# Spline layer of a graph network: features normalised singly, base weights held on chip, second half with banks and Silu buffer of its own, first half of the third norm moved ahead

## The reference

```python
def _layernorm(x, axis=-1, eps=1e-05):
    ...
def _L2_gnn_ref(h, W, a, base_w, spline_w, edge_index):
    ...
    att = ex / den[row]
    agg = jax.ops.segment_sum(att[:, None] * h[col], row, num_segments=N_NODES)
    grid = _grid()
    basis = _b_splines(agg, grid)
    out = jax.nn.silu(agg) @ base_w.T + jnp.einsum('nip,oip->no', basis, spline_w)
    return out
def _L3_gnn_ref(x, w, edge_index):
    ...
    message = jnp.concatenate([x, neighbor_mean], axis=-1)
    weighted = jnp.einsum('of,nf->no', w, message)
    return jax.nn.relu(weighted)
...
x = _layernorm(x + _L1_gnn_ref(...), axis=-1)
x = _layernorm(x + _L2_gnn_ref(x, ...), axis=-1)
x = _layernorm(x + _L3_gnn_ref(x, L3_gnn_w, edge_index), axis=-1)
```

## Time and profile before

| | |
|---|---|
| median of 3 runs | 1746.64 us (1743.93 to 1747.52) |
| the profiled execution | 1744.53 us, its span 1742.6 us |
| PE busy | 1470.6 us, 84% |
| DVE busy | 1321.9 us, 76% |
| ACT busy | 727.0 us, 42% |
| POOL busy | 499.8 us, 29% |
| mean granted clock of TensorE | 0.932 |

### The profile page before, as it was taken

One profiled execution on the slowest core, in us unless ns is written; L12 is line 12 of the kernel. 1 busy time (PEld: TensorE's weight loads), 2 busy tenths in 40 slices (PEclk: granted clock), 3 DMA queues, 4 the chain that ended last, 5 costly groups with the idle time before them and its releaser, 6 DMA issues.

```text
span 1742.6 us, 24098 instructions
## 1 busy us (share of the span) xinstructions
PE 1470.6 (84%) x7759; PEld 794.3 (46%) x7759; DVE 1321.9 (76%) x2036; ACT 727.0 (42%) x1595; POOL 499.8 (29%) x490
## 2 busy tenths in 40 slices
PE   2888998174878783799999999869899989999997
PEld 1465545022433332655655555745444434444443
DVE  8796999968999998499998999788377357724232
ACT  1285664075555553455554555431244134312000
POOL 1788888700010001255665664000000000002000
PEclk9889998587999996899999999979999999999999
DMA  4101000143120201455665666001011121210000
GB/s 150 31 6 9 6 6 6 35 144 87 55 73 30 72 15 39 136 169 172 189 182 166 180 190 123 1 0 49 0 58 62 48 73 48 72 72 0 12 18 29
DMA packets 67195, 122.74 MB, mean 70 GB/s; under 512 B 12613, under 2 KB 31159, under 8 KB 67010
## 3 DMA queue, kind: packets, MB, share of 16 engines
q0 software_dynamic: 22944, 58.12, 13.3%
q1 hardware_dynamic: 42748, 59.87, 10.6%
q10 hardware_dynamic: 1446, 4.03, 0.7%
HBM read 106.57 MB, written 15.22 MB: 70 GB/s over the span
## 4 chain that ended last, share of the span: by engine, by line
PE 48%; DVE 19%; POOL 14%; issue 11%; ACT 4%; DMA 3%; DVEq 1%; SPq 0%; ACTq 0%; another core or an unknown queue 0%; POOLq 0%
PE PS L1175 18%; POOL recs L641 14%; PE PS L1060 7%; DVE arena L1811 6%; PE PS L1223 5%; PE PS L1143 5%; PE PS L1046 4%; DVE arena L1807 3%; ACT arena L1486 2%; PE PS L1219 2%; PE PS L1211 2%; DVE arena L1775 2%; DVE arena L1947 1%; PE PS L1111 1%; DVE cnt_d L1581 1%
## 5 line engine op out<-in xcount | busy, mean ns | idle before, releaser
L1175 PE MATMUL PS<-arena 128*125 128x512 f32 x720 | 314.4, 600 | 12.1 <-ACT arena L1545 6.6
L641 POOL DMA_INDIRECT recs<-arena x170 | 249.0, 1464 | 90.6 <-issue 90.0
L1486 ACT ACTIVATE arena<-arena,gslot 128x32 f32<-128x32 f32 x832 | 185.3, 308 | 170.9 <-DVE arena L1930 81.6
L1060 PE MATMUL PS<-arena 128*32 128x128 f32 (+1 forms) x3328 | 231.3, 308 | 18.4 <-issue 7.9
L688 POOL DMA_INDIRECT arena<-xup,gidx x208 | 197.6, 950 | 141.8 <-DVE arena L1939 62.0
L1060 PEld LDWEIGHTS PS<-arena 128*32 128x32 f32 x3328 | 174.5, 110 | 127.5 <-issue 73.3
L977 PE MATMUL PS<-arena 125*128 125x512 f32 (+1 forms) x480 | 190.6, 535 | 44.0 <-DVE arena L1811 44.0
L1175 PEld LDWEIGHTS PS<-arena 128*125 128x125 f32 x720 | 136.8, 190 | 189.2 <-issue 189.2
L1939 DVE TENSOR_TENSOR arena<-PS,arena 128x768 f32<-128x768 f32 x208 | 196.7, 946 | 0.0
L695 POOL CAST arena<-cnt_s 125x1250 f32<-125x1250 uint16 x10 | 12.6, 1303 | 495.3 <-PE PS L1175 495.3
L977 PEld LDWEIGHTS PS<-arena 125*128 125x128 f32 x480 | 86.1, 192 | 148.5 <-issue 78.2
(11 more groups left out here) (311 smaller groups left out, 2008.2 us busy)
## 6 DMA issues: line engine op xcount, KB each, us to landing
arena<-in_spline_wT SPq DMA_DIRECT2D x16, 1024.0 KB, 5.3
arena<-uv_rows SPq DMA_DIRECT2D x14, 610.4 KB
arena<-h_rows SPq DMA_DIRECT2D x26, 256.0 KB
h_rows<-arena SPq DMA_DIRECT2D x24, 256.0 KB, 2.8
arena<-xup,gidx POOLq DMA_INDIRECT x208
recs<-arena POOLq DMA_INDIRECT x170
xup<-arena SPq DMA_DIRECT2D x10, 250.0 KB
out<-x_sb SPq DMA_DIRECT2D x10, 250.0 KB
```

The lines of the kernel that those rows point to most:

```text
L641: pool.indirect_dma_start(out=recs, out_offset=bass.IndirectOffsetOnAxis(pos[:, c:c + 1], 0), in_=rec[:, c, :], in_offset=None).then_inc(s ...
L1060: ins = t.matmul(PS[quad * DB:(quad + 1) * DB, bank, o0 * MUL:o0 * MUL + w], sel4[:, s, v * DB:(v + 1) * DB], prod[:, s, c0 * MUL:c1 * MUL ...
L1175: ins = t.matmul(PS[:NP, b, :], basis[:, slot, (k * HB + b) * NP:(k * HB + b + 1) * NP], w_sp[:, slot, k * D:(k + 1) * D], start=(first an ...
L1486: ins = A(sel4[:, s, y * DB:(y + 1) * DB], eq4[:, m // 4, s * DB:(s + 1) * DB], ACT.Copy, scale=gslot[:, par, c + R_Y + y:c + R_Y + y + 1])
```

## The change

In the aggregation, ScalarE copies groups 0 to 2 straight into `aggT`, and VectorE multiplies each there as it comes. Group 3 is not copied: VectorE reads it from PSUM, in two halves of the nodes. The Silu of the first half comes in two parts, three groups and then the last.

The base weights get a place of their own, `base_w`, in the memory of the count matrix `cnt_d`, and are loaded once. The first base product runs over the groups outside and the blocks inside, the second the other way round. The basis slots and the Silu of the second half (`silu_at[1]`) have places of their own; the second Silu waits for no step of TensorE any more. The first half sums in banks 3 to 7, the second in banks 0 to 4 (`y2_bank`), and TensorE waits at the fourth block of the second base product for two adds. VectorE's adds of the first half stand behind the first basis of the second half. Its eight steps are written out without a loop.

The first five blocks are normalised behind the last basis. The fourth layer's transposes use banks 7 and 6, its first products banks 5 and 0, and `w_l3` is loaded in two parts.

```diff
@@ -111,7 +111,9 @@
 
 
         x_sb = sb("x_sb", [NP, NB, D])
-        cnt_d = sb("cnt_d", [NP, NB * SPAN], u16)
+        cnt_all = sb("cnt_d", [128, NB * SPAN], u16)
+        cnt_d = cnt_all[:NP, :]
+        base_w = cnt_all[:, 0:2 * KT * D].bitcast(f32)
         cnt_s = sb("cnt_s", [NP, NB, N], u16)
         gld = sb("gld", [128, 2, TP * RW])
         gpk = sb("gpk", [1, 2, G // 2], i32)
@@ -267,21 +269,21 @@
...
-        aggr = at(16600, [128, KT, N])
+        aggT = at(16600, [128, KT, N])
         rden2 = at(21700, [128, N])
         Psum = at(25500, [NP, N])
-        aggT = at(0, [128, KT, N])
-        basis = at(5000, [128, 2, KT * HB * NP])
         w_sp = at(12500, [128, 2, KT * D])
-        sv, sa, sbb, sa2, sb2 = (at(o, [128, KT * HB * NP]) for o in (10000, 16600, 19100, 21600, 24100))
+        basis_at = [at(o, [128, KT * HB * NP]) for o in (27000, 5000)]
+        silu_at = (basis_at[0], at(7500, [128, KT * HB * NP]))
+        sv, sa, sbb, sa2, sb2 = (at(o, [128, KT * HB * NP]) for o in (10000, 0, 2500, 21600, 24100))
...
-        w_l3 = at(0, [128, 2 * KT, D])
+        w_near, w_self = at(16600, [128, KT, D]), at(0, [128, KT, D])
...
-        z_sb = at(16700, [NP, NB, D])
-        fin = at(21900, [NP, 2, D])
-        xT3 = at(23200, [128, KT, N])
+        z_sb = at(18700, [NP, NB, D])
+        fin = at(2100, [NP, 2, D])
+        xT3 = at(24000, [128, KT, N])
...
@@ -478,6 +480,9 @@
...
 
+        def y2_bank(half, b):
+            return (b + 3 + 5 * half) % 8
...
 
@@ -579,20 +584,30 @@
...
             sp.wait_ge(s_p2_ok, NB)
             spl = a["spline_wT"].rearrange("q (k p) n -> q p k n", p=128)
-            for half in range(2):
-                sp.wait_ge(s_sp_free, 10 * half + 1)
-                sp.dma_start(w_sp[:, 0, :].rearrange("p (k n) -> p k n", k=KT), kview(a["base_wT"])).then_inc(s_wsp_in0, 16)
...
-            sp.wait_ge(s_silu_ok, 2)
+
+            def spline_weights(q, slot):
+                sp.dma_start(w_sp[:, slot, :].rearrange("p (k n) -> p k n", k=KT),
+                             spl[bass.ds(q, 1), :, :, :].rearrange("q p k n -> (q p) k n"))\
+                  .then_inc(s_wsp_in0 if slot == 0 else s_wsp_in1, 16)
+            spline_weights(0, 1)
+            sp.wait_ge(s_psum_ok, NB)
+            sp.dma_start(base_w.rearrange("p (k n) -> p k n", k=KT), kview(a["base_wT"])).then_inc(s_wl2_in, 16)
+            spline_weights(1, 0)
+            with sp.Fori(0, NSPL // 2 - 1) as i:
+                for par in range(2):
+                    sp.wait_ge(s_sp_free, i * 2 + (par + 3))
+                    spline_weights(i * 2 + (par + 2), 1 - par)
+            with sp.Fori(0, NSPL // 2) as i:
+                for par in range(2):
+                    sp.wait_ge(s_sp_free, i * 2 + (NSPL + par + 1))
+                    spline_weights(i * 2 + par, 1 - par)
+
...
-            sp.dma_start(w_l3, kview(a["w_l3T"])).then_inc(s_wl3_in, 16)
+            sp.dma_start(w_near, wl3[1]).then_inc(s_wl3_in, 16)
+            sp.wait_ge(s_basis_ok, 2 * NSPL)
+            sp.dma_start(w_self, wl3[0]).then_inc(s_wl2_in, 16)
...
@@ -690,7 +705,7 @@
...
-            pool.wait_ge(s_sp_free, 2 + 2 * (NSPL + 1))
+            pool.wait_ge(s_sp_free, 2 + 2 * NSPL)
             for k in range(NB):
                 pool.tensor_copy(cnt50[:, k, :], cnt_s[:, k, :]).then_inc(s_p3_ok, 1)
 
@@ -1169,54 +1184,70 @@
             pe.wait_ge(s_psum_ok, NB)
             all_parts(3, 0)
 
-            def spline_step(slot, first, last):
+            def spline_product(half, b, k, lhs, w, first):
+                return t.matmul(PS[:NP, y2_bank(half, b), :], lhs[:, (k * HB + b) * NP:(k * HB + b + 1) * NP],
+                                w[:, k * D:(k + 1) * D], start=(first and k == 0), stop=False, skip_group_check=True)
+
+            def spline_step(half, i, par):
+                slot = 1 - par
+                pe.wait_ge(s_wsp_in0 if slot == 0 else s_wsp_in1, i * 16 + 16 * (4 * half + 1))
+                pe.wait_ge(s_basis_ok, i * 2 + (NSPL * half + par + 1))
                 for b in range(HB):
                     for k in range(KT):
-                        ins = t.matmul(PS[:NP, b, :], basis[:, slot, (k * HB + b) * NP:(k * HB + b + 1) * NP],
-                                       w_sp[:, slot, k * D:(k + 1) * D], start=(first and k == 0), stop=(last and k == KT - 1),
-                                       skip_group_check=True)
+                        ins = spline_product(half, b, k, basis_at[slot], w_sp[:, slot, :], False)
                 ins.then_inc(s_sp_free, 1)
-            for half in range(2):
-                if half:
-                    pe.wait_ge(s_y2_cp, HB)
-                pe.wait_ge(s_wsp_in0, 16 * (5 * half + 1))
...
-                        spline_step(slot, False, False)
-
-            for b in range(NB + 1):
-                if b < NB:
-                    pe.wait_ge(s_x_ok, 2 * NB + b + 1)
-                    if b >= 1:
-                        pe.wait_ge(s_xt3_cp, b)
...
+            pe.wait_ge(s_wl2_in, 48)
+            pe.wait_ge(s_silu_ok, 1)
+            for k in range(KT):
+                if k == KT - 1:
+                    pe.wait_ge(s_silu_ok, 2)
+                for b in range(HB):
+                    ins = spline_product(0, b, k, silu_at[0], base_w, True)
+            ins.then_inc(s_sp_free, 1)
+            with pe.Fori(0, NSPL // 2) as i:
+                for par in range(2):
+                    spline_step(0, i, par)
+            pe.wait_ge(s_silu_ok, 3)
+            for b in range(HB):
+                if b == 3:
+                    pe.wait_ge(s_y2_cp, 2)
+                for k in range(KT):
+                    spline_product(1, b, k, silu_at[1], base_w, True)
+            with pe.Fori(0, NSPL // 2) as i:
+                for par in range(2):
+                    spline_step(1, i, par)
+
+            def x3_transposes(b):
+                pe.wait_ge(s_x_ok, 2 * NB + b + 1)
+                if b >= 2:
+                    pe.wait_ge(s_xt3_cp, b - 1)
+                for k in range(KT):
+                    ins = t.transpose(PS[:, 7 - b % 2, k * 128:k * 128 + NP], x_sb[:, b, k * 128:(k + 1) * 128], ident[:NP, :NP])
+                ins.then_inc(s_xt3_ps, 1)
+
+            x3_transposes(0)
+            x3_transposes(1)
+            for c in range(NB):
+                pe.wait_ge(s_xt3_cp, c + 1)
+                if c == 0:
+                    pe.wait_ge(s_wl3_in, 16)
+                if c == 1:
+                    pe.wait_ge(s_y2_cp, HB + 1)
+                if c >= 2:
+                    pe.wait_ge(s_z_cp, c - 1)
...
+                if c + 2 < NB:
+                    x3_transposes(c + 2)
             pe.wait_ge(s_z_cp, NB)
+            pe.wait_ge(s_wl2_in, 64)
...
@@ -1530,19 +1561,24 @@
...
-            for b0, f, done in ((0, 0, 1), (3, 1, 2), (3, 2, 4), (0, 3, 5)):
+            for b0, f, done in ((0, 0, 1), (3, 1, 2), (3, 2, 4)):
                 act.wait_ge(s_l2_agg, done)
-                A(aggr[:, f, :], PS[:, b0:b0 + 3, :].rearrange("p a n -> p (a n)")[:, 0:N], ACT.Copy).then_inc(s_l2_cp, 1)
+                A(aggT[:, f, :], PS[:, b0:b0 + 3, :].rearrange("p a n -> p (a n)")[:, 0:N], ACT.Copy).then_inc(s_l2_cp, 1)
 
             HW = HB * NP
...
             for half in range(2):
                 av = aggT[:, :, half * HW:(half + 1) * HW]
...
-                act.wait_ge(s_aggT_ok, half + 1)
-                act.wait_ge(s_sp_free, 10 * half + 1)
-                A(as3(basis[:, 0, :]), av, ACT.Silu).then_inc(s_silu_ok, 1)
+                if half == 0:
+                    act.wait_ge(s_aggT_ok, KT - 1)
+                    A(as3(silu_at[0])[:, 0:KT - 1, :], av[:, 0:KT - 1, :], ACT.Silu).then_inc(s_silu_ok, 1)
+                    act.wait_ge(s_aggT_ok, KT)
+                    A(as3(silu_at[0])[:, KT - 1, :], av[:, KT - 1, :], ACT.Silu).then_inc(s_silu_ok, 1)
+                else:
+                    act.wait_ge(s_aggT_ok, KT + 1)
+                    A(as3(silu_at[1]), av, ACT.Silu).then_inc(s_silu_ok, 1)
                 with act.Fori(0, NSPL // 2) as i:
...
@@ -1554,8 +1590,21 @@
...
             def z_out(b):
                 act.wait_ge(s_z_ps, b + 1)
-                A(z_sb[:, b, :], PS[:NP, 5 + b % 2, :], ACT.Copy).then_inc(s_z_cp, 1)
-            evac_T(xT3, s_xt3_ps, s_xt3_cp, (7, 7), 3, z_out)
+                A(z_sb[:, b, :], PS[:NP, 5 * (1 - b % 2), :], ACT.Copy).then_inc(s_z_cp, 1)
+
+            def x3_in(b):
+                act.wait_ge(s_xt3_ps, b + 1)
+                A(xT3[:, :, b * NP:(b + 1) * NP],
+                  PS[:, 7 - b % 2, :].rearrange("p (k n) -> p k n", k=KT)[:, :, 0:NP], ACT.Copy).then_inc(s_xt3_cp, 1)
+            for b in range(HB):
+                ln_sqrt(3, b)
+            for b in range(NB):
+                x3_in(b)
+                if b < HB:
+                    ln_sqrt(3, HB + b)
+                if b >= 1:
+                    z_out(b - 1)
+            z_out(NB - 1)
...
@@ -1991,7 +2040,7 @@
...
```

(66 more changed lines are left out.)

62 lines of the change are left out of this document (15 added, 47 removed).

## The result

The changed kernel takes 1723.54 us in the median of 4 runs (1722.15 to 1727.07), the kernel before 1747.08 (4 runs, 1743.93 to 1748.0). The ratio is 0.9881 with a 95% interval of 0.9859 to 0.9902, that is 17.1 to 24.6 us less. In another batch of runs, in which the kernel before took 1718.25, the ratio was 0.9883 (0.9851 to 0.9915). The forecast was 1726.9 in a range of 1722.5 to 1733.5.

A forecast was written before the change was run, and what follows sets the result against it. The prediction took TensorE's chain, with its pauses and the slower clock behind them, as the bound. Terms 6.60 + 2.37 + 5.46 + 3.15 + 2.1 = 19.7 us came off the 1746.64 median: 1726.9, range 1722.5 to 1733.5.

The forecast's parts named there:

- The three pauses: TensorE's stops between aggregation and splines (6.60 us), between spline halves (5.46), and before the fourth layer's first product (3.48).
- first pause: TensorE's 6.60 us stop between aggregation and splines, forecast to go, with 2.37 us of slower clock behind it.
- The clock: With no idle ahead of either spline half, TensorE's clock stays at 1.00, giving back 2.37 and 3.15 us.
- Rival A: The low clock is not tied to the pauses and comes anyway: 5.52 us stay, 1732.4 us; chance 0.11.
- The fourth feature: After the aggregation, VectorE's PSUM reads and a partial Silu finish during 15 base products, ready near T + 1.5 us.
- The first basis: Ready 16.7 to 16.8 us after the last aggregation matmul, needed at 17.16; cost 0, bounds 0 and 1.3 us.
- Bank order: The first base product changes banks with every matmul; cost taken as 0, as in the aggregation's rows.
- The third norm: Normalising the first half's blocks behind the last basis starts the fourth layer's products sooner: 2.1 us less, bounds 0 and 2.9.
- keep ahead: After the splines, VectorE's work on the other half's blocks stays ahead of TensorE's 3.87 us per block.
- third pause: The 3.48 us between splines and the fourth layer's first product; 1.63 us idle before its first transpose, clock 1.00 after.
- rival B: A late first basis (1728.2 us) or an unseen wait of 3 us or so at a handover (1730); chance 0.08.
- the base weights' part: One early load, own banks and own Silu buffer remove the stop between the spline halves: 5.46 us less.

The follow-up runs named there:

- x4: The change with its first part undone: ScalarE copies the fourth feature too, VectorE multiplies all four afterwards, one Silu per half; ratio to the kernel before 0.9912.
- x5: Same as x4, but TensorE works off 7 unused products while it waits for the Silu; ratio to the kernel before 0.9926.
- x9: Same as x1, but TensorE works off 3 unused products while it waits; ratio to the kernel before 0.9883.
- x1: The change, with TensorE waiting for all five adds of the first half before the second half's base product; ratio to the kernel before 0.9904.
- x2: The change, with base weights loaded again for the second half, only once TensorE has finished the first half; ratio to the kernel before 0.9925.
- x8: The change, with 3 unused products before the aggregation and the last z copy's wait behind four products needing no z; ratio to the kernel before 0.9873.
- x11: Same as x8 with 4 unused products in place of 3; ratio to the kernel before 0.9859.
- x6: The change, with all sixteen spline steps ordered features outside, blocks inside, so every matmul changes bank; ratio to the kernel before 0.9864.
- x7: The change, with the first five blocks normalised only after TensorE finishes the splines, all five before the adds; ratio to the kernel before 0.9894.
- x10: Same as x7, but with the other blocks' adds and statistics placed between the normalisations; ratio to the kernel before 0.9886.
- x3: The change, with the base weights loaded a second time as in x2, but issued one spline step earlier; ratio to the kernel before 0.9871.

## Why the prediction was right

*The three pauses.* 12.06 us of pause and 5.52 of clock were forecast to go, and 17.46 of 17.58 did. Each part alone gives its price back: the first 9.6 (forecast 6.60 + 2.37 = 8.97), the second, as a late load, 8.7 (forecast 8.61), the third 2.2 (forecast 2.1). Together these are 20.5 against 19.63; most of the difference is the clock's share of the first pause, 0.7 more in x4 than in the kernel before.

*The clock.* This was the step that a reader of the chain alone would have missed, a quarter of the gain. x5 and x9 show it to come from TensorE's idle time, by one trace each. The other traces agree: all five idle pauses of 3.26 us or more at the splines (two before, one each in x4, x1 and x2) have the lower clock behind them, and no trace without a pause there has it. Rival A (0.11) is out. The 5.52 of the sum are not all clock, though. With the clock kept at 1.00, a start behind a wait still took 0.24 to 0.26 us more (x5, x9, and x8 and x11 with 42.28 against 42.02), so some 0.5 of the 5.52 come from stopping at all. Closing the pauses gave back both.

*The fourth feature.* VectorE's two instructions took 1.52 us (forecast 1.64) and the last part of the Silu ended at 1243.20, T + 1.60 (forecast 1.5), over 11 us before TensorE asked. The base weights' load was issued at 1203.28, 38 us ahead of T (forecast over 20).

*The first basis.* Ready at T + 16.67 against a forecast of 16.7 to 16.8, and the race was won as forecast. What the step left out is that the load of the stationary operand is due 0.43 us before its matmul; that load was late by 0.15 us, and the lead absorbed it.

*Bank order.* Cost 0 was taken from the aggregation's rows, and the first base product ran at 1.00 (the stretch from 1243.30). x6 confirms it for sixteen steps more. Against it stood the Trainium skill, "TensorE: Matmul & The Clock Gate", section "A second HAM failure mode: psum-queue depth-cycling" (the prediction names the section ahead of it), which tells of a bfloat16 kernel that went through the banks, idled briefly between its groups of matmuls and had its clock fall again and again. No such idling shows in this case's float32 products: 309.00 us busy of 309.00 in x6.

*The third norm.* 2.26 against 2.1. The first transposes took 0.44 us of the chain and not 0.65, the handovers 0.06 and not 0.15. The sentence that the other blocks "keep ahead" was right for the change; in x7, where VectorE comes to them later, it was not. That the clock stays up behind the third pause was true of the trace before and of x10, but not of x7, so in some executions the third pause can cost more than the 2.9 that the term allowed.

*What was wrong.* The statement under rival B that a pause of 3 us "is too short by the third pause's example to lower the clock". x1 shows 3.26 us of idle costing 1.9 us more. The third pause consisted of 1.63 and 0.77 us with transposes between them, and was no bound for 3 us in a row; in x7 the clock fell even behind a pause of that kind. Rival B's price for a 3 us wait should have been about 5, 1732 in place of 1730. And the account of what the base weights' part gains, "from one load", was loose: x3 shows that a second load is free if it goes out a step earlier.

The measured median lies 3.4 us under the forecast, and 1.0 us above the range's lower end; one of its four runs lies below that end. Behind T the sum was right to 0.1 us. The rest lies ahead of T or in the scatter of runs, which reach over 4.9 us for the change. The sum has no term for what lies ahead of T, so that the median stayed in the range was in part luck.

## What to carry to other kernels

On a chain that one engine carries, list its pauses in the chain of waits and price each with the slower clock behind it: here 12 us of idle cost 17.5. If such a pause can't be closed, work that nobody needs, put into it on TensorE, gave back most of the clock's share in the traces (2.80 us in x5, 1.75 in x9), too little for the timed runs here to show. And a load that hurts wants an earlier start before it wants to be saved.

## What the runs showed of the hardware

- A float32 product of 125x512 shows as two instructions of 0.429 us each at a granted clock of 1.00, whichever bank the one before went to.
- TensorE's clock behind idle time: 3.26 us of idle in a row cost 1.9 us more (x1), 5.46 and 5.53 us cost 3.15 each (before, x2), 6.6 us cost 2.4 and 3.1 (before, x4), and the 5 us ahead of the aggregation cost 1.4 to 3.1 over twelve traces. 1.63 and 0.7 us with transposes between cost none before and in x10, but in x7 the clock fell behind them, and eight instructions took 5.29 in place of 3.60 us.
- A start behind a wait takes 0.24 to 0.26 us more even at a clock of 1.00 (x5, x8, x9, x11). This is part of the losses above, those ahead of the aggregation excepted.
- The fall can come late: in x1 the clock was 1.00 for over a microsecond after TensorE had started again, and then 0.50 in the stretches from 1377.00, at full work.
- Work that serves nothing keeps the clock up as other work does (x5, x8, x9, x11).
- In this stream TensorE's load of a stationary operand comes one spacing, 0.43 us, ahead of its matmul. One that was 0.15 us late (1258.33) did not delay TensorE.
